# A causal mask on VectorE instead of TensorE, in the attention stage of a one-layer language model on one core

## The reference

```python
def _attn(q, k, v, causal):
    scale = 1.0 / math.sqrt(q.shape[-1])
    s = jnp.einsum('bhqd,bhkd->bhqk', q, k) * scale
    if causal:
        Tq, Tk = (s.shape[-2], s.shape[-1])
        mask = jnp.tril(jnp.ones((Tq, Tk), dtype=bool))
        s = jnp.where(mask, s, jnp.finfo(s.dtype).min)
    return jnp.einsum('bhqk,bhkd->bhqd', jax.nn.softmax(s, axis=-1), v)

a1 = _attn(q, k1, v1, causal=True)      # latent
a2 = _attn(q, ks, vs, causal=False)     # select
a3 = _attn(q, kw, vw, causal=True)      # window
out = g[:, 0] * a1 + g[:, 1] * a2 + g[:, 2] * a3
```

## Time and profile before

| | us |
|---|---|
| median of 3 runs | 2747.41 |
| lowest and highest | 2745.13, 2747.56 |
| profiled execution | 2745.16 |
| its span, first to last instruction | 2743.4 |

### The profile page before, as it was taken

One profiled execution on the slowest core, in us unless ns is written; L12 is line 12 of the kernel. 1 busy time (PEld: TensorE's weight loads), 2 busy tenths in 40 slices (PEclk: granted clock), 3 DMA queues, 4 the chain that ended last, 5 costly groups with the idle time before them and its releaser, 6 DMA issues. The chain is left out here.

```text
span 2743.4 us, 38402 instructions
## 1 busy us (share of the span) xinstructions
PE 2327.9 (85%) x12402; PEld 1845.8 (67%) x12402; DVE 1815.3 (66%) x2824; ACT 1743.7 (64%) x3574; POOL 1622.2 (59%) x1430
## 2 busy tenths in 40 slices
PE   0178579999999999999999999999999997538885
PEld 0155346777777777777777777777777775538885
DVE  2557457686776868687776868677686773455553
ACT  3433226777777777777777777777778776116663
POOL 4055316667676666767676666766656665006885
PEclk9985569999999999999999999999999998759998
DMA  9757654325151533414251533232132110615776
GB/s 382 311 187 246 189 127 108 91 68 136 24 154 29 136 66 108 112 48 124 52 142 38 138 69 91 61 67 60 34 67 49 32 25 17 194 62 177 197 203 169
DMA packets 199860, 314.87 MB, mean 115 GB/s; under 512 B 95915, under 2 KB 130219, under 8 KB 186731
## 3 DMA queue, kind: packets, MB, share of 16 engines
q1 hardware_dynamic: 189947, 298.23, 37.9%
q0 software_dynamic: 9712, 14.18, 2.8%
HBM read 210.20 MB, written 101.75 MB: 114 GB/s over the span
## 5 line engine op out<-in xcount | busy, mean ns | idle before, releaser
L1392 POOL TENSOR_TENSOR p_lo<-prob,p_hi 128x512 fp32r<-128x512 f32 (+2 forms) x960 | 1092.3, 1145 | 630.0 <-ACT p_hi L1473 544.7
L1471 ACT ACTIVATE prob<-ps_s 128x512 f32<-128x512 f32 (+4 forms) x1344 | 722.8, 538 | 465.8 <-PE ps_s L1489 303.0
L1607 DVE TENSOR_REDUCE max_part<-ps_x 128x1 f32<-128x128 f32 (+1 forms) x1240 | 713.4, 606 | 195.9 <-PE ps_x L1518 128.0
L1473 ACT ACTIVATE p_hi<-ps_s 128x512 fp32r<-128x512 f32 (+3 forms) x1344 | 718.5, 535 | 1.6
L1392 DVE TENSOR_TENSOR p_lo<-prob,p_hi 128x512 fp32r<-128x512 f32 (+1 forms) x320 | 308.0, 962 | 129.8 <-ACT p_hi L1473 124.4
L1575 PE MATMUL ps_o<-p_hi,v_win 128*128 128x512 f32 (+3 forms) x640 | 251.9, 394 | 8.5 <-DVE p_lo L1392 8.5
L1575 PE MATMUL ps_o<-p_hi,v_lat 128*128 128x512 f32 (+3 forms) x640 | 242.6, 379 | 0.0
L1577 PE MATMUL ps_o<-p_lo,v_win 128*128 128x512 f32 (+3 forms) x640 | 234.6, 367 | 0.0
L1577 PE MATMUL ps_o<-p_lo,v_lat 128*128 128x512 f32 (+3 forms) x640 | 234.1, 366 | 0.0
L1668 DVE TENSOR_TENSOR raw_o<-ps_o,low_sum 32x512 f32<-32x512 f32 x192 | 131.4, 684 | 78.9 <-ACT low_sum L1456 74.5
L1518 PE MATMUL ps_x<-k_hi,head_first 96*128 96x512 f32 (+2 forms) x320 | 120.6, 382 | 29.0 <-DVE max_part L1607 28.0
(11 more groups left out here) (432 smaller groups left out, 5830.9 us busy)
## 6 DMA issues: line engine op xcount, KB each, us to landing
raw<-in_experts_w_dram SPq DMA_DIRECT2D x23, 1536.0 KB
wbuf<-in_tok_weight_dram SPq DMA_DIRECT2D x16, 2000.0 KB, 16.9
head_first<-kw_scratch SPq DMA_DIRECT2D x72, 256.0 KB, 4.7
kw_scratch<-st_hi SPq DMA_DIRECT2D x48, 256.0 KB, 2.8
kw_scratch<-st_lo SPq DMA_DIRECT2D x48, 256.0 KB, 3.3
q_scratch<-st_hi SPq DMA_DIRECT2D x48, 256.0 KB, 4.8
q_scratch<-st_lo SPq DMA_DIRECT2D x48, 256.0 KB, 5.5
head_first<-q_scratch SPq DMA_DIRECT2D x48, 256.0 KB, 7.5
```

The costliest lines, as they stand in the source:

```text
L1392: ns.tensor_tensor(upper if low else p_lo[:, i % LSLOTS, c:CH], prob[low:P, i % NPROB, c:CH], upper.bitcast(F32), ALU.subtract).then_inc(s ...
L1471: nc.scalar.activation(prob[low:P, i % NPROB, c:CH], ps_s[i % 3][low:P, c:CH], ACT.Exp, scale=SCALE).then_inc(s["p_full"], 1)
L1473: nc.scalar.activation(p_hi[:, i % SLOTS, c:CH], ps_s[i % 3][:, c:CH], ACT.Exp, scale=SCALE).then_inc(s["p_up"], 1)
L1607: ins = nc.vector.tensor_reduce(mpart[:, q, c:c + 1], bank[:, 0:w], axis=AX.X, op=ALU.max)
```

## The change

TensorE no longer adds the triangle, neither in the score bank nor in the maxima bank of `attend`. Instead VectorE does, at two places. In each diagonal unit it waits for the scores, adds `mask_kq` to 128 columns of the score bank in place, and raises a new semaphore, `cut`; ScalarE's exponential of a diagonal unit waits for `cut` instead of `scores`. In a diagonal maximum, one combined instruction adds a row of zeros ending in the triangle (`before`, a new constant of 512 columns) to the bank and takes the maximum; it is followed by an instruction that stores the result.

```diff
+            cst.add(nc.gpsimd.memset(g.before[:], 0.0))
...
+            cst.add(nc.gpsimd.affine_select(out=g.before[:, CH - P:CH], in_=g.before[:, CH - P:CH], compare_op=ALU.is_ge, fill=MASKED,
+                                            base=0, pattern=[[-1, P]], channel_multiplier=1))
...
+DIAG = [i for i in CAUSAL if UNITS[i][2] >= 4 * UNITS[i][1]]
...
-                    wait_unit(act, "scores", h, i)
+                    if i in DIAG:
+                        act.wait_ge(s["cut"], len(DIAG) * h + DIAG.index(i) + 1)
+                    else:
+                        wait_unit(act, "scores", h, i)
...
-                    diag = c == q // 4
                     last = nc.tensor.matmul(bank[:, 0:w], q_hi[par][0:DQK, q * P:(q + 1) * P], k_hi[b][par][0:DQK, c * CH:c * CH + w],
-                                            start=True, stop=not diag)
-                    if diag:
-                        last = nc.tensor.matmul(bank[:, w - P:w], g.ident16[:], g.mask_qk[:], start=False, stop=True)
+                                            start=True, stop=True)
...
-            mid = (lambda: nc.tensor.matmul(bank[:, col:col + P], g.ident16[:], g.mask_kq[:], start=False, stop=False)) if diag else None
...
-                    ins = nc.vector.tensor_reduce(mpart[:, q, c:c + 1], bank[:, 0:w], axis=AX.X, op=ALU.max)
+                    if c == q // 4:
+                        ins = nc.vector.tensor_tensor_reduce(bank[:, 0:w], bank[:, 0:w], g.before[:, CH - w:CH], 1.0, -3.0e38, ALU.add, ALU.max, mpart[:, q, c:c + 1])
+                    else:
+                        ins = nc.vector.tensor_reduce(mpart[:, q, c:c + 1], bank[:, 0:w], axis=AX.X, op=ALU.max)
...
+                    if i in DIAG:
+                        wait_unit(dve, "scores", h, i)
+                        c = width(i)[0]
+                        cut = ps_s[i % 3][:, c:c + P]
+                        nc.vector.tensor_tensor(cut, cut, g.mask_kq[:], ALU.add).then_inc(s["cut"], 1)
                     for t in AT.get((h, i), ()):
                         dve_task(dve, t)
```

More of the change, by code:

```diff
@@ L1105, in attend @@
         s = {k: ctx.enter_context(nc.semaphore("h_" + k)) for k in
-             ("scores", "p_full", "p_up", "lo_pool", "lo_dve", "pv", "x", "x_read", "turn", "back", "full", "up", "low_dve", "low_pool", "nmax", "nmax_t",
+             ("scores", "p_full", "p_up", "lo_pool", "lo_dve", "cut", "pv", "x", "x_read", "turn", "back", "full", "up", "low_dve", "low_pool", "nmax", "nmax_t",
               "o_read", "s_read", "low0", "low1", "sums", "inv", "inv_st", "weight", "norm", "done", "store", "set", "ones", "gset", "k1r",
@@ L1554, in pe_scores @@
             col, _ = width(i)
-            diag = b != SELECT and k >= 4 * j
             wait_unit(pe, "p_up", h, i - 3)
@@ L1558, in pe_scores @@
             bank = ps_s[i % 3]
-            mid = (lambda: nc.tensor.matmul(bank[:, col:col + P], g.ident16[:], g.mask_kq[:], start=False, stop=False)) if diag else None
             aug = DQK + b + 1
-            three(bank[:, col:CH], k_hi[b][par][0:aug, ks], k_lo[b][par][:, ks], q_hi[par][0:aug, qs], q_lo[par][:, qs], mid, DQK).then_inc(s["scores"], 1)
+            three(bank[:, col:CH], k_hi[b][par][0:aug, ks], k_lo[b][par][:, ks], q_hi[par][0:aug, qs], q_lo[par][:, qs], rows=DQK).then_inc(s["scores"], 1)
         def pe_values(pe, h, i):
@@ L2318, in layer @@
         g.gates, g.onehot, g.inv = tile("gates", [P, 3]), tile("onehot", [QA, NB]), tile("inv", [P, 1])
+        g.before = tile("before", [P, CH], BF16)
         with ExitStack() as mid:
```

## The result

| | before | changed |
|---|---|---|
| median of 4 runs, us | 2746.27 | 2681.17 |
| lowest and highest, us | 2742.26, 2747.56 | 2674.85, 2684.76 |
| ratio | | 0.9763, 95% interval 0.975 to 0.9776 |

The change takes 65 us away, 2.4% of the time.

The account below looks back on a forecast made before the run. TensorE was taken to bound most of a head, VectorE units 21 to 38. Gains of 19 us (heads 0 to 11), 10 (heads 12 to 14) and 1.2 (last head) gave -31 us: 2716, range 2685 to 2785.

Parts of the forecast that it names:

- the middle: Units 7 to 38 of a head's 84; VectorE 95% busy from unit 21, TensorE's saving worth nothing there.
- The price of a product: Each mask product removed from TensorE saves 0.13 us, 0.12 for maxima, 0.03 for 128 wide scores; 113 us in all.
- the latent stretch: Units 44 to 83 of a head, bound by TensorE: shrinks from 52.2 us to 48.5 to 49.5.
- the opening: Units 0 to 6 of a head, bound by TensorE; with units 39 to 83 it loses 4.3 us of products.
- The cut and the combined maximum: VectorE's added work: 0.25 us per score bank addition, 0.05 more per diagonal maximum; 9.6 us a head.
- the allowance for the row of diagonal units 44 to 47: Exponentials there stand behind VectorE too: 0.7 us a head lost, so 3.6 of 4.3 counted.
- The middle, +2.0: Units 7 to 38, heads 0 to 11: new work and waits 3.8 us, 1.8 into existing waits, so 2.0 longer.
- The output's wait: VectorE's output sum waits for ScalarE's copy behind the delayed exponential; around units 22 and 23, some 0.75 us later.
- The whole saving arrives: Rival: TensorE's whole saving outside units 7 to 38 counts, at most 74 us, giving 2673; chance 0.08.
- The locks at 2747 and 2780: Rivals: VectorE's backlog delays TensorE at four diagonal units a head, 0.5 us each (2747) or 1 us (2780); chance 0.15 each.
- The combined maximum at half rate: Rival: VectorE's add-and-max costs 0.33 us more than a reduce, not 0.05; 80 us, giving 2796; chance 0.12.
- half of the way: Reason given for the range's lower end, 2685: halfway to the whole saving outside units 7 to 38, and a little more.

Follow-up runs that it names:

- run c: Kernel before with TensorE's mask products removed and nothing in their place, so no mask in the attention loops; ratio 0.975.
- run e: Kernel before with VectorE's subtractions and closing products and sums replaced by one-operand passes of the same size; ratio 0.978.
- f: Changed kernel with VectorE's subtractions and closing products and sums replaced by one-operand passes of the same size; ratio 0.9649 to the kernel before.
- run d: Changed kernel with TensorE's mask products kept as well, so each mask is applied twice; ratio 0.9981 to the kernel before.

## Why the prediction was off

**What bounds the kernel.** Right outside the middle: in run c TensorE's stretches there shrank by 3.9 us a head, against the 4.3 of its products. Wrong in the middle: 95% busy was read as 95% of work. In units 21 to 38 a part of it was standing still for GpSimd, and without that (run e) the middle is TensorE's.

**The price of a product.** Right. 0.13, 0.12 and 0.03 give 3.36 us for the latent stretch, measured 3.41. Of the 4.3 us outside the middle that leaves 0.94 for the opening and units 39 to 43. The opening gave 0.51 in run c; units 39 to 43 gave 0.4 in the seventh head, but nothing on average over heads 1 to 11 (7.47 against 7.45).

**The cut and the combined maximum.** 0.25 was taken for the cut; it lasts 0.30 and takes 0.20 behind another instruction, the lower bound. The combined maximum was to cost 0.05 more than a reduce and cost 0.01, its store nothing. "Below 0.8 with its read" holds (0.69 + 0.14 overlapped).

**The latent stretch.** 48.5 to 49.5 was forecast, 49.55 measured. Of the 3.4 us of its products 0.7 were lost, and 0.7 was the allowance for the row of diagonal units 44 to 47. It was lost at that place: from the last score product of unit 46 to that of unit 47 the changed kernel takes 1.82 us, run c 1.11, and all other units of the stretch together differ by 0.01. Units 39 to 43 gave nothing either: 7.68 us on average, 7.80 in the head shown. Outside the middle the changed kernel so keeps 3.0 us a head, where 3.6 were forecast.

**The middle, +2.0: the step that failed.** With the collisions taken away it is +2.0 (e to f), by another balance than the one that was worked out. With them it was -0.5 in heads 1 to 11, and in heads 12 to 14 -3.0, against a forecast of +0.15 (their units 7 to 20 at -1.0 and 21 to 38 at +1.15; measured +0.1 and -3.0, and in run c, without the new work, -0.9 and -0.2). The working took the durations of the profile before as given, and added the new work and the new wait to them. But the durations of two-operand instructions were themselves the outcome of a phase, which the new wait changed: a subtraction takes 848 ns instead of 981, and the collisions, which cost 60 us before, cost 31. By heads: the 11 gained 3.4 each instead of 1.6 (20 us of the difference), heads 12 to 14 5.8 instead of 3.45 (7 us), the first head 8.5 instead of 1.6 (7 us). The first head also gains 6.8 between e and f and 8.4 in run c, so its gain needs neither collisions nor the new work, and the missing products suffice for it; why they are worth so much there is open. In the two profiled executions attention ends 67 us earlier in the changed kernel and what follows it, which the change does not touch, takes 5 us more; that is not explained.

**The output's wait.** It was forecast that VectorE's output sum of unit 23 waits 0.75 longer. It waits 1.31 us against 0.82: the direction is right, and it stands on the path only as part of the +2.0.

**The rivals.** "The whole saving arrives" gave 2673 and lies nearest in number, but not as it was argued: outside the middle the changed kernel keeps 3.0 us a head of 4.3, and the rest comes from the middle, which had no part in that rival. The locks at 2747 and 2780 did not come about: with TensorE's products kept (run d), the wait and the work together gave back 5 us instead of costing any. The combined maximum at half rate is ruled out by 693 ns. No case covered a change of the collisions; with one, the range would have had to reach to about 2650, the time of f. (Its lower end of 2685 was also not "half of the way" to 2673: half is 2694.)

## What to carry to other kernels

Before an engine's busy share is taken as its load, compare the longest and the shortest duration of the same instruction: a subtraction of 512 columns that takes 0.68 or 1.60 us is partly a wait that the page counts as work. Where VectorE and GpSimd both run two-operand instructions on SBUF, count who starts second, and expect a new wait that ties one of them to a third engine to change that count. A range for such a change must take in the whole price of the collisions, here about 60 us, which one run with one-operand passes measured.

## What the runs showed of the chip

- A two-operand subtraction of 512 columns from SBUF on VectorE took 0.68 us alone. If GpSimd was in a two-operand instruction when it began, it ended 0.55 us after GpSimd's (225 of 243 in the kernel before within 0.01 us; the one shown took 1.60). Where VectorE had begun first, GpSimd's took 1.48 to 1.57 in place of 1.29 us on average. A one-operand pass of the same size on VectorE took 0.67 to 0.69 us throughout.
- VectorE adds in place in PSUM over 128 columns in 0.30 us, 0.20 from start to start; the combined add and maximum over 512 columns from PSUM and SBUF takes 0.69 (the plain reduce 0.69), and the store of its result (0.14) overlaps with the next instruction.
- A semaphore that VectorE raises by an instruction of its own comes ahead of the work in hand (at 282 of 512 places the engine was in the middle of an instruction): ScalarE waited at most 1.2 us for it, against 3.2 us where an addition raised it.
